# Image loads, the token difference, the resize products and the order of four engines in a window-attention kernel

## The reference, cut to what matters

```python
def window_attn(x, Wqkv, bqkv, scale, ws=2, nh=8):      # windows of 2x2 tokens, 8 heads of 16
    qkv = (xw @ Wqkv + bqkv).reshape(B, hg * wg, ws * ws, 3, nh, hd)
    attn = softmax(einsum('bgnqd,bgnkd->bgnqk', q, k) * scale, axis=-1)
    o = einsum('bgnqk,bgnkd->bgnqd', attn, v)
...
xr = x.reshape(B, H, W, C)                               # x: (4, 128, 32, 32)
g = window_attn(xr, Wqkv, bqkv, scale) @ Wproj + bproj
l = l.reshape(B, C, H // 2, 2, W // 2, 2).mean(axis=(3, 5))
l = window_attn(l.reshape(B, h, w, C), Wqkv, bqkv, scale)
lx = 0.5 * (px[:, :, :-1, :] + px[:, :, 1:, :])
ly = 0.5 * (py[..., :-1] + py[..., 1:])
l = jax.image.resize(lx + ly, (B, C, H, W), method='bilinear')
...
x = x + _L0_conv_ref(_gn(x), ...)                        # _gn: group norm, 32 groups of 4 channels
```

## Time and profile before

| what | value |
|---|---|
| median of 3 runs | 80.9 us (80.78 to 81.19) |
| the profiled execution's own time | 80.81 us |
| its span, first to last instruction | 79.1 us |
| PE busy | 70.1 us, 89% of the span |
| DVE, POOL, ACT busy | 58.6, 54.3, 39.2 us |
| share of PE in the chain that ended last | 81% |
| share of DMA in that chain | 8% |

### The profile page before, as it was taken

One profiled execution on the slowest core, in us unless ns is written; L12 is line 12 of the kernel. 1 busy time (PEld: TensorE's weight loads), 2 busy tenths in 40 slices (PEclk: granted clock), 3 DMA queues, 4 the chain that ended last, 5 costly groups with the idle time before them and its releaser, 6 DMA issues.

```text
span 79.1 us, 1517 instructions
## 1 busy us (share of the span) xinstructions
PE 70.1 (89%) x524; PEld 53.8 (68%) x524; DVE 58.6 (74%) x89; ACT 39.2 (50%) x73; POOL 54.3 (69%) x79
## 2 busy tenths in 40 slices
PE   0994697999999999999999999999999999999500
PEld 0493497645655577684678657989599999899300
DVE  0015936899997997999799999999699998333600
ACT  0070030647967798666387675646365736370100
POOL 5917841990958258499899899999996619982000
PEclk9999999999999999999999999999999999999999
DMA  0899999100000000000000000000000000009385
GB/s 0 240 229 237 249 256 274 41 0 0 0 0 12 0 0 0 0 0 12 0 4 0 0 0 0 0 8 0 0 0 0 0 8 0 0 31 365 135 320 210
DMA packets 2375, 5.21 MB, mean 66 GB/s; under 512 B 832, under 2 KB 1088, under 8 KB 2368
## 3 DMA queue, kind: packets, MB, share of 16 engines
q1 hardware_dynamic: 1760, 3.74, 15.5%
q10 hardware_dynamic: 608, 1.38, 6.9%
HBM read 3.02 MB, written 2.10 MB: 65 GB/s over the span
## 4 chain that ended last, share of the span: by engine, by line
PE 81%; DMA 8%; DVE 2%; issue 1%; ACTq 1%; DVEq 1%
PE q_ps L756 12%; PE s_ps L795 9%; PE k_ps L747 9%; PE v_ps L773 8%; DMA x_sb<-in_x 8%; PE job_ps L831 7%; PE ot_ps L809 7%; PE job_ps L848 5%; PE job_ps L724 5%; PE q_ps L854 3%; PE v_ps L770 3%; PE k_ps L831 3%; PE k_ps L848 2%; PE v_ps L711 2%; PE s_ps L831 1%; PE v_ps L724 1%
## 5 line engine op out<-in xcount | busy, mean ns | idle before, releaser
L424 POOL TENSOR_TENSOR pv<-pv 128x512 f32<-128x512 f32 x18 | 22.9, 1273 | 3.8 <-DVE pv L658 3.3
L600 DVE TENSOR_TENSOR qk<-q_sb,k_ps 128x1536 f32<-128x1536 f32 x10 | 17.3, 1729 | 0.2 <-PE k_ps L747 0.2
L658 DVE TENSOR_TENSOR pv<-prob_w,v_ps 128x1536 f32<-128x1536 f32 x9 | 15.6, 1735 | 0.0
L557 DVE BATCH_NORM_STATS2 bn<-x_sb 128x6 f32<-128x512 f32 x8 | 5.4, 686 | 7.7 <-DMA x_sb<-in_x 7.7
L756 PE MATMUL q_ps<-xt,w_sb 128*128 128x512 f32 x16 | 9.2, 662 | 0.0
L535 ACT COPY ot<-ot_ps 128x512 f32<-128x512 f32 x9 | 5.3, 585 | 7.3 <-PE ot_ps L809 7.3
L498 ACT ACTIVATE q_sb<-q_ps,bias_qkv 128x512 f32<-128x512 f32 x10 | 6.8, 682 | 3.8 <-PE q_ps L756 3.6
L747 PE MATMUL k_ps<-xd,w_sb 128*128 128x384 f32 x20 | 8.6, 516 | 0.0
L773 PE MATMUL v_ps<-w_sb,xd 128*128 128x128 f32 x60 | 8.3, 275 | 0.0
L795 PE MATMUL s_ps<-qk,head_sum 128*32 128x192 f32 x160 | 7.5, 329 | 0.0
L773 PEld LDWEIGHTS v_ps<-w_sb,xd 128*128 128x128 f32 x60 | 7.5, 192 | 0.0
(11 more groups left out here) (92 smaller groups left out, 127.3 us busy)
## 6 DMA issues: line engine op xcount, KB each, us to landing
out<-out_sb SPq DMA_DIRECT2D x3, 512.0 KB, 2.6
x_sb<-in_x SPq DMA_DIRECT2D x4, 256.0 KB, 6.9
x_sb<-in_x ACTq DMA_DIRECT2D x4, 256.0 KB, 7.3
resize_sb<-in_resize SPq DMA_DIRECT2D x1, 640.0 KB, 8.8
out<-out_sb SPq DMA_DIRECT2D x1, 256.0 KB, 3.4
out<-out_sb ACTq DMA_DIRECT2D x1, 256.0 KB, 3.5
w_sb<-in_L_conv_Wqkv SPq DMA_DIRECT2D x1, 192.0 KB, 7.6
wp_sb<-in_L_conv_Wproj ACTq DMA_DIRECT2D x1, 64.0 KB, 9.6
```

The costliest lines, as they stand in the source:

```text
L424: nc.gpsimd.tensor_tensor(first, first, other, ALU.add).then_inc(summed[i], 1)
L600: nc.vector.tensor_tensor(qk[:, m % 2, :, :, n % 2, :], q, k, ALU.mult).then_inc(qk_done, 1)
L658: nc.vector.tensor_tensor(to, p, v, ALU.mult).then_inc(pv_done, 1)
```

## The change

1. **Loads.** SP issues each image whole, and also the output weights. ACT issues no load. `x_loaded[b]` counts to 16.
2. **Token 0 subtracted from PSUM.** For tiles 0 and 1 DVE reads the three other tokens from the PSUM bank of the transpose instead of from the copy in SBUF; token 0 still comes from the copy, so the wait is the same. The transpose `("xt", 0, 1)` goes to the bank `k_ps[1]` instead of `job_ps`.
3. **Resize.** Two middle columns take their pooled tokens from a new tile `middle`: its partitions 0 to 63 come from the pooled half 1, its partitions 64 to 127 from the pooled half 0, and the resize block is composed to match. So each column is one product, four for a half image instead of five. `middle` is filled by ACT (new step `mid`, four copies of 64x128 for each pooled tile), and every `low` step waits for it ahead of its first product. The resize matrix has eight blocks instead of ten.
4. **The denominator** of the fifth pair on DVE is one reduction instead of two additions.
5. **Warm-up.** `WARM` becomes `(4, 2)`, `(1,)`, `(2, 2)`: one matmul of 512 and one of 256 columns ahead of `("mean", 0)`, and two of 256 ahead of `("mean", 1)`.
6. **The order** of all four engines is rewritten. `TILES` is as it was: the second pooled tile stands at index 6 of the list, counted from 0, in both kernels.

```diff
-    used = [(k, l) for k in range(K) for l in range(KL) if r[l, :, k].any()]
-    return used, np.stack([r[l, :, k] for k, l in used], 1).astype(np.float32)
+    for k in range(K):
+        part = 2 if k in MIDDLE else k // WIN
+        block = np.concatenate([r[1, :64, k], r[0, 64:, k]]) if part == 2 else r[part, :, k]
...
-WARM = {("mean", 0): 5, ("var", 0): 1, ("mean", 1): 5}
+WARM = {("mean", 0): (4, 2), ("var", 0): (1,), ("mean", 1): (2, 2)}
...
+            if job == ("xt", 0, 1):
+                return k_ps[1]
...
-            for b in range(2):
-                sp.dma_start(x_sb[0:64, b, :], x_chan[b, 0:64]).then_inc(x_loaded[b], 16)
-            sp.dma_start(w_sb[:, :], w_qkv).then_inc(w_loaded, 16)
-            for b in range(2, B):
-                sp.dma_start(x_sb[0:64, b, :], x_chan[b, 0:64]).then_inc(x_loaded[b], 16)
+            for b in range(B):
+                sp.dma_start(x_sb[:, b, :], x_chan[b]).then_inc(x_loaded[b], 16)
+                if b == 1:
+                    sp.dma_start(w_sb[:, :], w_qkv).then_inc(w_loaded, 16)
...
-            for b in range(B):
-                act.dma_start(x_sb[64:128, b, :], x_chan[b, 64:128]).then_inc(x_loaded[b], 16)
-            act.dma_start(wp_sb[:, :], w_proj).then_inc(wp_loaded, 16)
...
+            def middle_part(p):
+                low = TILES.index((None, p))
+                act.wait_ge(ot_out, low + 1)
+                parts = ot[:, low, :].rearrange("f (e h i a x) -> f i h a e x", e=2, h=2, i=2, a=8)
+                for half in range(2):
+                    at = slice(64 * half, 64 * (half + 1))
+                    for i in range(2):
+                        ins = nc.scalar.copy(middle[at, p, i, :].rearrange("f (a e x) -> f a e x", a=8, e=2),
+                                             parts[at, i, 1 - half])
+                    ins.then_inc(middle_out, 1)
...
-                less_token_0(nc.vector, n).then_inc(diff_dve, 1)
+                less_token_0(nc.vector, n, bank(("xt", *TILES[n]))).then_inc(diff_dve, 1)
...
-                    nc.vector.tensor_tensor(key_pairs[:, 1, :], e[:, 0:128], e[:, 128:256], ALU.add).then_inc(pairs_dve, 1)
-                    dve.wait_ge(pairs_dve, done)
-                    nc.vector.tensor_tensor(denom[:, m % 2, :], key_pairs[:, 1, 0:64], key_pairs[:, 1, 64:128],
+                    nc.vector.tensor_reduce(denom[:, m % 2, :], by_window(expd[:, m % 2, :]), AX.X,
...
+                pe.wait_ge(middle_out, 2 * nth("ACT", ("mid", b // 2)))
...
-                for i in used:
-                    column, half = BLOCKS[i]
-                    nc.tensor.matmul(view[:, column % 4], resize_sb[:, i, :], parts[:, b % 2, half],
-                                     start=(i == used[0]), stop=True, skip_group_check=True)
+                for t in range(WIN):
+                    part = PARTS[WIN * k + t]
+                    nc.tensor.matmul(view[:, t], resize_sb[:, WIN * k + t, :], shared if part == 2 else parts[:, part],
+                                     start=(t == 0), stop=True, skip_group_check=True)
```

73 lines of the change are left out of this document (41 added, 32 removed), and 36 rows, old and new, of the table ORDER.

## The result

The changed kernel takes 73.2 us (median of 4 runs, 73.0 to 75.7) against 80.8 us (4 runs of the kernel before beside them). The ratio is 0.904, with a 95% interval of 0.900 to 0.908: 7.6 us less, where 3.7 were forecast. The profiled execution took 73.2 us, with a span of 71.5 and the same 1.7 us outside.

What follows compares the result with a forecast made beforehand. Loads bound the start, PE the middle with DVE close behind, stores the end. Span 79.1 - 0.6 - 0.5 + 0.3 - 1.8 + 0.4 - 1.4 = 75.5, plus 1.7 outside, gives 77.2 us; range 76.0 to 79.3.

Steps and rivals of the forecast that it cites:

- Loads, -0.6: At the start: images 0 and 1 through one queue land sooner, a gain of 0.6 us, bounds 0 and 1.2.
- The cover of that step: At the start: image 2, which kept DVE until 11.93, must land 0.6 us sooner too, and does at the middle rate.
- The clock, +0.3: At the start: PE's rise to 2.4 GHz comes earlier with the work or at the same moment; 0.3 us lost, bounds 0 and 0.6.
- Warm-up, -0.5: Ahead of the mean of image 1: 512 columns instead of 640 on the path, 1.87 us for 2.34, a gain of 0.5.
- Token difference, 0: DVE's two differences for tiles 0 and 1: 0.85 us less each from PSUM, worth 0 on the path.
- Resize, -1.8: PE between 49 and 72 us: eight half images lose one product of 0.22 us each, 1.8 us, all on the chain.
- New waits, +0.4: Waits from the new order at the fill, DVE's tile 6 and POOL: 0.8 us together, taken as 0.4, bounds 0 and 1.8.
- The wait of DVE at tile 6: In the middle: K 6 ends at 40.1, DVE would be there at 39.8, so DVE waits 0.3 us.
- Tail, -1.4: At the end: the last store lands 2.1 us after its issue instead of 3.5, a gain of 1.4.
- (a): At the loads: one queue buys nothing, image 1 lands at 8.0 as now, 78.1 us; chance 0.14.
- (b): In the middle: DVE and POOL become the bound, PE stalls by what the resize products free, 79.0 us; chance 0.13.
- (c): At the start: PE stays at the low clock level longer, slower, 82.7 us if low until the first score sum; chance 0.05.

Runs made afterwards that it cites:

- after_again: The changed kernel once more, unchanged: 73.0 us (72.9 to 75.9), ratio 0.911 to the kernel before; its profile is of a run of 75.9 us.
- a_oldloads: The changed kernel with the old loads, half images on two queues: 78.1 us (77.2 to 78.4), ratio 0.970 to the kernel before.
- b_warm: The kernel before with the new warm-up alone: 80.4 us (79.7 to 81.0), ratio 1.000 to the kernel before.
- a_midwait: The changed kernel, with PE waiting for `middle` only ahead of the shared product, made last of four: 73.0 us (72.7 to 75.7); profiled run 75.7.
- a_ten: The changed kernel with ten resize blocks and five products as before, without `middle`: 74.2 us (74.1 to 78.1), ratio 0.925 to the kernel before.
- b_loads: The kernel before with the new loads alone, including SP's load of the output weights: 77.1 us (75.2 to 79.0), ratio 0.939 for its two lower runs.
- a_sbufdiff: The changed kernel with the token difference read from SBUF alone, as before: 74.0 us (72.7 to 76.0), ratio 0.908 to the kernel before.
- b_bn_warm: The kernel before with DVE's first statistics of images 2 and 3 moved later and more warm-up columns: 78.0 us (77.9 to 78.1), ratio 0.968.

## Why the prediction was wrong

The measured 73.2 us lies below the stated range, 76.0 to 79.3. Two steps failed, both in the start: the loads, taken at -0.6 us and measured at about -2.1, and the clock level, taken at +0.3 and measured at about -2.5. The second is the larger, and its sign was wrong. By its own steps:

- **Loads, -0.6 with bounds 0 and 1.2: too small.** The upper bound was taken from one microsecond in which the resize matrix moved 317 GB/s, read as what one queue does. It was a whole transfer over 128 partitions against two halves, and the slices went to 294 to 368. Image 1 came 2.5 us earlier, image 2 2.9. The rate was called nearer to the slices of before because of the queues that alternated; the runs say that the rate has nothing to do with queues. Arrival by itself measured 2.0 to 2.1 us.
- **The cover of that step.** The prediction asked that image 2 land 0.6 us sooner as well, and took it as given. It is the path of the changed kernel, and in after_again the late image 2, with the level lost behind it, cost 2.7 us. It was a wait in the start that a step of DVE could have moved, and I had named it as cover instead of pricing it.
- **The clock, +0.3 with bounds 0 and 0.6: the wrong sign.** It knew two cases, the level rises sooner with the work, or at the same moment. The runs show a third: the first warm-up can raise the level by itself, long before the first queries. With the old loads this was lost again around the two means (a_oldloads, b_warm); with the images sooner, and less idle time between the warm-ups, it is kept. In the trace of before it could only have been suspected: the warm-up took 2.34 us at the low level, directly before the low transposes, and I took the low level up to 17.55 as given. Measured against a_oldloads: 2.1 us from the transposes to the first keys, and 0.9 in the warm-up itself. Against the kernel before: 5.3 us from the first transposes to the end of the first keys became 3.6, and the warm-up gave 0.9 beyond its fewer columns, 2.5 to 2.6 in all. Why the level rose in the first warm-up of one execution and not in that of another (after and a_midwait, on the same program up to there) stays open, and so it is in part luck that the profiled one had it; three of its four runs have that time.
- **Warm-up, -0.5:** as a change of its own between -0.4 and +0.5 (b_warm). The shortening was real in the chain; it bought nothing while the level was low at the same place. First transposes forecast for 12.2, measured 9.82.
- **Token difference, 0:** right on the path. The operation went from 1.34 us to 0.56 and 0.50, but the reason was read wrongly: from SBUF alone it took 0.51 and 0.56 as well where POOL stood idle.
- **Resize, -1.8:** right in size in the chain, 0.89 for 1.12 us seven times, the first 1.13 where it had been 1.23. Net of the fill and its wait, 1.1 by times and up to 1.7 by ratios (a_ten).
- **New waits, +0.4 with bounds 0 and 1.8:** measured as 55.7 - 1.8 = 53.9 against 54.5, so +0.6. They stand where they were looked for only in part. The forecast 0.2 at the fill is 0.08 + 0.27 idle; 0.2 more is at 39.73 and 0.1 at the keys at 16.96. The wait of DVE at tile 6, which was to be 0.3, is not there. PE was idle for 0.35 us of the 33 between 31 and 64.
- **Tail, -1.4:** 1.3, in size right. The last store landed 2.1 us after its issue, as written. Image 2's, issued at 66.42 and landed at 69.0, still ran beside it for 0.6 us, which the prediction had named as a sign of being wrong; it cost nothing that shows.
- **The range:** its low end came from a sum said to reach 75.9 with the load at 1.2 and no waits. Those two give 77.2 - 0.6 - 0.4 = 76.2, and 75.9 only with the clock's +0.3 taken off too. It had no term for a level that comes early.

Of the rivals, (a) fell: the loads did change the rate. (b) fell: PE did not stall by what the products freed. (c) had the right mechanism with the opposite sign. It asked what happens if PE's level comes later, priced that at one us for each us of work, and gave the case 0.05; that it could come earlier by the same price was left to the 0.04 under 76.

What stays open: how much the rewritten order of the four engines is worth by itself. Between the two lower runs of b_loads (75.3) and the changed kernel (73.1) lie 2.2 us. The resize products are 1.1 to 1.7 of them and the tail 1.3, so that the rest of the order comes to a loss of 0.2 to 0.8; this is a difference of other numbers, it takes the level to be the same in both, and no run isolates it.

## What to carry to other kernels

A matmul piece that takes twice its later time is a price list by itself: ask what idle time of PE stands ahead of it, and whether the change closes or opens that, before a constant is put for the level. When a load gets faster, write down which image the engine behind it waits for next, and whether a step of the list has that wait ahead of work that is needed sooner; with two steps of statistics moved and one gap of 0.5 us closed, none of six runs was near 75.5 us, which is a hint and no proof. When an operation is timed for use in another place, ask what ran beside it: the difference of token 0 took 0.5 or 1.3 us from the same operands, by what POOL did. And a transfer rate is to be read together with the partitions that each transfer spans.

## What the runs showed of the hardware

- Between 2 and 8 us, half images (64 partitions) moved 235 GB/s over two queues and 249 over one, whole images 368 over two and 348 over one (338 in the changed kernel).
- DVE's subtraction of 128x384 from SBUF took 0.51 and 0.56 us with POOL idle (a_sbufdiff, b_bn_warm), 1.34 and 1.45 beside POOL's pooling sums (before, a_sbufdiff), and 0.50 beside them with one input in PSUM (the changed kernel).
- The granted clock fell from the full to the half level in the start, behind idle time of PE around the means, and stayed there into work without a gap: in a_oldloads the first queries took 1.96 us behind transposes that followed each other directly. In other executions it had not risen in the first warm-up at all (a_midwait: 2.05 us for the columns that took 1.11). Two executions of the changed kernel differ by 2.7 us by a fall of the level and by the landing of one image, at 8.33 or 9.50 us. The Trainium skill, "TensorE: Matmul & The Clock Gate", says of the start that the moment of the rise varies from run to run, and puts its cost at under 1% of a typical span; the moment does vary here, but the low stretch and the late image took 3.7% of 73 us together in after_again, 1.5 of the 2.7 us by the level, and in a_midwait the level took 2.8 us by itself.
- The page can print a full clock all along while the pieces of the chain show half speed; in other executions it prints the fall. The durations decide.
